# Cross-attention by pairs of feature chunks, with the null key taken out of the keys

## The reference, cut to what matters

```python
q = split_heads(layernorm(x) @ Wq) * DH ** -0.5
k, v = split(ctx @ Wkv)                      # then split_heads
k = concat(null_k, k); v = concat(null_v, v) # 129 keys
attn = softmax(q @ k.T)
out = merge_heads(attn @ v) @ Wout           # then a layer norm with scale and bias
x = x + tanh(g_xattn) * out
```

## Time and profile before

| | |
|---|---|
| runs | 588.56 us median of 3 (588.01 to 589.29) |
| profiled execution | span 586.1 us (its own device time is not listed apart from the runs) |
| TensorE matmul | 532.3 us busy, 91% |
| VectorE | 405.8 us busy, 69% |
| ScalarE | 308.6 us busy, 53% |
| GpSimd | 123.5 us busy, 21% |
| prologue | 0 to 50.7 us |
| groups 0 to 5 | 50.1 us each |
| group 6 | 42.0 us |
| group 7 | 39.1 us |
| feed-forward block | 432.5 us to the end |

### The profile page before, as it was taken

The page is one execution under the profiler, slowest core; times in us unless marked ns, Lnnn a source line. Parts: engine busy times, 40 slices in busy tenths (PEclk is TensorE's granted clock), DMA queues, the critical chain, the costliest instruction groups (busy, mean ns, idle before and its releaser), DMA issues. The chain is left out here.

```text
span 586.1 us, 11057 instructions
## 1 busy us (share of the span) xinstructions
PE 532.3 (91%) x3972; PEld 460.8 (79%) x3972; DVE 405.8 (69%) x1054; ACT 308.6 (53%) x880; POOL 123.5 (21%) x129
## 2 busy tenths in 40 slices
PE   2899999999999999999999999999678999807897
PEld 2888888888988998888898888887466878704797
DVE  4669844755574575466457447947785888999896
ACT  2744532643353363344335326425678659989992
POOL 3000310220130122022103102302303108940000
PEclk9999999999999999999999999999999999957999
DMA  7932001100110110010011001001300100010033
GB/s 243 350 127 73 2 1 55 37 2 3 52 36 0 54 36 0 20 41 28 0 54 36 0 1 37 1 2 56 107 19 2 36 0 2 0 36 1 1 102 115
DMA packets 18479, 25.88 MB, mean 44 GB/s; under 512 B 1216, under 2 KB 15808, under 8 KB 18448
## 3 DMA queue, kind: packets, MB, share of 16 engines
q1 hardware_dynamic: 18192, 25.17, 13.1%
q0 software_dynamic: 256, 0.30, 0.3%
HBM read 21.27 MB, written 4.19 MB: 43 GB/s over the span
## 5 line engine op out<-in xcount | busy, mean ns | idle before, releaser
L834 ACT ACTIVATE probs<-bank,nmax 128x129 f32<-128x129 f32 x256 | 91.0, 369 | 117.9 <-DVE nmax L1196 117.8
L1625 POOL TENSOR_TENSOR probs<-probs,rinv 128x512 f32<-128x512 f32 x64 | 66.7, 1043 | 339.0 <-DVE rinv L1204 339.0
L615 PE MATMUL bank<-wv,ctxT 128*128 128x512 f32 x384 | 94.3, 397 | 0.0
L607 PE MATMUL bank<-ctxT,wk 128*128 128x256 f32 x672 | 88.9, 282 | 0.0
L615 PEld LDWEIGHTS bank<-wv,ctxT 128*128 128x128 f32 x384 | 70.4, 188 | 17.0 <-issue 1.2
L607 PEld LDWEIGHTS bank<-ctxT,wk 128*128 128x128 f32 x672 | 83.6, 188 | 0.0
L1208 DVE COPY pT<-bank 128x512 f32<-128x512 f32 x64 | 43.7, 683 | 20.6 <-PE bank L678 18.7
L815 ACT ACTIVATE oT<-bank 128x256 fp32r<-128x256 f32 x64 | 24.8, 387 | 59.9 <-PE bank L687 59.9
L607 PE MATMUL bank<-xnT,wq 128*128 128x256 f32 x336 | 54.7, 298 | 0.0
L834 ACT ACTIVATION_READ_ACCUMULATOR probs<-bank,nmax 128x1 f32 x256 | 52.0, 203 | 0.0
L607 PEld LDWEIGHTS bank<-xnT,wq 128*128 128x128 f32 x336 | 43.2, 188 | 7.2 <-issue 1.2
(11 more groups left out here) (177 smaller groups left out, 846.5 us busy)
## 6 DMA issues: line engine op xcount, KB each, us to landing
craw<-in_ctx SPq DMA_DIRECT2D x8, 512.0 KB, 3.3
stage<-in_L_xattn_Wkv SPq DMA_DIRECT2D x8, 512.0 KB, 13.1
xa<-in_x SPq DMA_DIRECT2D x8, 256.0 KB, 2.7
xr<-in_x SPq DMA_DIRECT2D x8, 256.0 KB, 2.7
x_scratch<-y SPq DMA_DIRECT2D x7, 256.0 KB, 2.1
x2all<-x_scratch SPq DMA_DIRECT2D x1, 1792.0 KB, 8.4
xres<-x_scratch SPq DMA_DIRECT2D x6, 256.0 KB, 2.8
out<-yout SPq DMA_DIRECT2D x6, 256.0 KB, 2.2
```

The source lines that it names most:

```text
L607: last = mm(bk[:, n * TG:(n + 1) * TG], wt[a][:, k, f], act_t[b][:, k, :], start=(k == 0 and i == 0), stop=(k == kk - 1 and i == len(TERMS ...
L615: last = mm(bk[:, :], ctxT[a][:, k, b * S:(b + 1) * S], wv[w][:, k, h * 512:(h + 1) * 512], start=(k == 0 and i == 0), stop=(k == KC - 1 a ...
L834: last = nc.scalar.activation(probs[:, c % 2, u, 0:NK], score_bank[c % 2][h][:, b * QW:b * QW + NK], ACT.Exp, bias=nmax[:, c % 2, u:u + 1] ...
L1625: G.tensor_tensor(probs[:, c % 2, :, 0:S], probs[:, c % 2, :, 0:S], rinv[:, c % 2, :].rearrange("p (u o) -> p u o", o=1).to_broadcast([P, ...
```

## The change

A **pair** of chunks takes the place of a chunk (`NP = 4` pairs in a group). The null key is subtracted from every key when ScalarE copies the keys out of PSUM, so the score of the null key is 0 for every query and needs no column: four score tiles of 128 columns fill one bank, and the eight tiles of a pair fill two. TensorE makes the scores of a pair in one batch of 16 matmul instructions, the values of a pair in one batch into the whole of `pv_bank`, and the transposes in two halves `h`, each of four tiles, through the one `pt_bank`. `maxima` becomes, for each half, a reduce over 512 columns and a minimum with 0 that waits for it; `exps` gets a fifth small activation (the exponential of the null key); `inverse_sums` becomes an addition and a reciprocal that waits for it. A `Q` unit makes the keys first, and ScalarE copies its two halves with one activation each, the keys' with a bias.

The units are dealt anew into four slots of three parts, `ahead`, `between` and `behind` the two halves of the transposes; a unit may be cut in two (`"Q4<"`, `"Q4>"`). The rest of VectorE's list moves from eight steps to four slots.

```diff
-    PLAN = ([["Q0"], ["Q1"], ["Q2"], ["Q3"], ["Q4"], ["Q5", "V00"], ["Q6", "V10"], ["Q7", "X"]],
-            ["V01", "V11", "C", "W"])
-    PLAN_PENULT = ([["Q0"], ["Q1"], ["Q2"], ["Q3"], ["Q4"], ["V00"], ["Q5"], ["Q6"]], ["V10", "W"])
-    PLAN_FINAL = ([["V01"], ["V11"], ["Q7", "F0"], ["F1"], ["F2"], ["F3"], ["F4"], ["F5", "F6"]],
-                  ["F7", "F8", "W"])
+    PLAN = (((["Q0"], ["Q1"], ["Q2"]), (["Q3"], ["Q4<"], ["Q4>"]), (["Q5"], ["Q6"], ["V00"]),
+             (["Q7"], ["V10<"], ["V10>", "X"])), ["V01", "V11", "C", "W"])
+    PLAN_PENULT = (((["Q0"], ["Q1<"], ["Q1>"]), (["Q2"], ["Q3<"], ["Q3>"]), (["Q4"], ["Q5<"], ["Q5>"]),
+                    (["V00"], ["V10<"], ["V10>"])), ["W"])
+    PLAN_FINAL = (((["Q6"], ["Q7<"], ["Q7>"]), (["V01<"], ["V01>"], []), (["V11<"], ["V11>"], ["F0"]),
+                   (["F1"], ["F2", "F3"], ["F4", "F5"])), ["F6", "F7", "F8", "W"])
...
             def prob_transposes(g, p, h):
+                n = 2 * (g * NP + p) + h
+                pe.wait_ge(norm_done, n + 1)
+                wait(pe, pt_copied, n)
...
             def values(g, p):
+                wait(pe, pt_copied, 2 * (g * NP + p) + 2)
+                wait(pe, ot_lo, g * NP + p)
...
             def group(g):      # TensorE
+                for p in range(NP):
+                    if has_next(g, p):
+                        scores(*after_pair(g, p))
+                    ahead, between, behind = slots[p]
+                    run(ahead)
+                    prob_transposes(g, p, 0)
+                    run(between)
+                    prob_transposes(g, p, 1)
+                    run(behind)
+                    values(g, p)
+                run([u for u in tail if u != "C"])
...
             def exps(g, p, h):      # ScalarE
+                nc.scalar.activation(null_exp[:, p % 2, h, :], nmax[:, p % 2, h, :], ACT.Exp).then_inc(exp_done, 1)
...
             def attention_stats(g, dst):      # VectorE
-                maxima(g + 1, 1)
+                maxima(g + 1, 1, 0)
                 ln2.wait()
...
                 last.then_inc(w_free, 1)
+                maxima(g + 1, 1, 1)
...
+            def maxima(g, p, h):
+                n = 2 * (g * NP + p) + h + 1
+                if h == 0:
+                    dve.wait_ge(scores_done, g * NP + p + 1)
+                V.tensor_reduce(nmax[:, p % 2, h, :], score_bank[p % 2][h][:, :].rearrange("p (u s) -> p u s", s=S),
+                                AX.X, ALU.max, negate=True).then_inc(keys_max, 1)
+                dve.wait_ge(keys_max, n)
+                V.tensor_scalar(nmax[:, p % 2, h, :], nmax[:, p % 2, h, :], 0.0, None, ALU.min).then_inc(max_done, 1)
+            def inverse_sums(g, p, h):
+                n = 2 * (g * NP + p) + h + 1
+                dve.wait_ge(exp_done, n)
+                V.tensor_tensor(rowsum[:, p % 2, h, :], rowsum[:, p % 2, h, :], null_exp[:, p % 2, h, :],
+                                ALU.add).then_inc(total_done, 1)
+                dve.wait_ge(total_done, n)
+                V.reciprocal(rinv[:, p % 2, h, :], rowsum[:, p % 2, h, :]).then_inc(rinv_done, 1)
...
             def group(g):      # VectorE
+                for p in range(NP):
+                    if p:
+                        if has_next(g, p):
+                            for h in range(2):
+                                maxima(*after_pair(g, p), h)
+                        out_low(g, p - 1)
+                    ahead, between, behind = slots[p]
+                    if p == 0 and not first:
+                        attention_rstd(g - 1)
+                        attention_norm(g - 1, y)
+                    if p == 1 and not first:
+                        x2_statistics(g - 1, y[:, :, :])
+                    if p == 1 and feeds(g):
+                        ln_stats(g + 2)
+                    if p == 2 and feeds(g):
+                        ln_rstd()
+                    if first and p == 0:
+                        weight_values(0)
+                    if first and 1 <= p:
+                        (weight_scales, weight_integers, weight_values)[p - 1](1)
+                    if peeled and g == NG - 2 and 1 <= p:
+                        (weight_scales, weight_integers, weight_values)[p - 1](2)
+                    run(ahead)
+                    prob_copy(g, p, 0)
+                    if has_next(g, p):
+                        inverse_sums(*after_pair(g, p), 0)
+                    run(between)
+                    prob_copy(g, p, 1)
+                    if p == 2 and feeds(g):
+                        ln_apply()
+                    if has_next(g, p):
+                        inverse_sums(*after_pair(g, p), 1)
+                    run(behind)
```

More of the change, by code:

```diff
@@ L87, in gated_cross_attention_ffn @@
     NT = B * S // P
-    QW = S + 2
-    NK = S + 1
+    NP = NS // 2
     NBK = I * D // P // WBLOCK
@@ L159, in parity, with whole, after_pair, has_next @@
         return (len(PRO) + pos) % 2
+    def whole(part):
+        return [u for u in part if u[-1] != "<"]
+    def after_pair(g, p):
+        return (g, p + 1) if p + 1 < NP else (g + 1, 0)
+    def has_next(g, p):
+        return p + 1 < NP or not (isinstance(g, int) and g == NG - 1)
     def feeds(g):
@@ L659, in unit, with scores @@
                             last.then_inc(w_first, 1)
[L660 to L667, removed]
+                if half != 0:
+                    last.then_inc(unit_done, 1)
+            def scores(g, p):
+                if isinstance(g, int) and g == NG - 1 and p == NP - 1:
+                    unit_read(g, FINAL.index("Q7"))
+                wait(pe, exp_done, 2 * (g * NP + p) - 2)
+                for u in range(4):
+                    c, b = 2 * p + u // GB, u % GB
@@ L693, in _, with run @@
                 if PRO[pos] == "k6":
-                    pe.wait_ge(null_ready, 1)
                     scores(0, 0)
             def group(g):
[L698 to L715, removed]
+                pos, (slots, tail) = 0, plan(g)
+                def run(part):
+                    nonlocal pos
+                    for u in part:
+                        unit(g, pos, "<>".index(u[-1]) if u[-1] in "<>" else None)
+                        pos += u[-1] != "<"
+                for p in range(NP):
[9 more added lines that the diff above has]
+                run([u for u in tail if u != "C"])
             group(0)
@@ L1278, in _ @@
                 if PRO[npos[0]] == "k6":
-                    maxima(0, 0)
-                    inverse_sums(0, 0)
+                    for h in range(2):
+                        maxima(0, 0, h)
+                    for h in range(2):
+                        inverse_sums(0, 0, h)
                 if PRO[npos[0]] == "V11":
@@ L1283, in _ @@
                 npos[0] += 1
-            maxima(0, 1)
+            for h in range(2):
+                maxima(0, 1, h)
             dve.wait_ge(const_ready, 1)
@@ L1360, in group, with run @@
+                pos, (slots, tail) = 0, plan(g)
+                def run(part):
+                    nonlocal pos
+                    for u in whole(part):
+                        if u == "C":
+                            ctx_low(g + 2)
+                            continue
                         split(g, pos)
                         pos += 1
-                    if c < NS - 1 and weights:
-                        inverse_sums(g, c + 1)
-                    if c < NS - 1:
-                        prob_copy(g, c)
@@ L1386, in group @@
+                out_low(g, NP - 1)
+                run(tail)
                 if not final:
@@ L1638, in group @@
                                         ALU.add).then_inc(xgb_ready, 1)
-                    normalise(g, c)
-                if not (isinstance(g, int) and g == NG - 1):
-                    normalise(g + 1, 0)
+                    if has_next(g, p):
+                        for h in range(2):
+                            normalise(*after_pair(g, p), h)
             group(0)
```

250 lines of the change are left out of this document (107 added, 143 removed).

## The result

The changed kernel takes 612.32 us (median of 4 runs, 611.46 to 613.5) beside 588.28 us for the kernel before on the same chip: a ratio of 1.043 with a 95% interval of 1.041 to 1.045. The forecast was 606.6 us in a range of 596 to 614.

The account below looks back on a forecast made before the run. TensorE's own list was taken as the bound. Prologue +2.2, group 0 +3.4, loop groups +8.3, group 6 +2.9 and group 7 +1.2 sum to +18.0 on 586.1; with 2.5 for the median, 606.6 us, range 596 to 614.

Parts of the forecast that it names:

- What bounds the kernel, and the gain: TensorE's list sets the time up to 393 us; batching shortens a loop group by 2.64 us to 47.46.
- A unit behind transposes: On TensorE, a unit following transposes has no switch cost; bound 0.1 us each, 64 times, 6 us.
- The late copy: VectorE's first pT copy holds TensorE's second transposes: 2.1, 1.6, 0.6 us in slots 0, 1, 2; some 35 in all.
- The linked minimum: VectorE's minimum behind each reduction costs 0.21 us, a half 0.81; by the skill some 0.1 less.
- The waits of 2 us cost nothing in clock: TensorE's new waits leave the granted clock at 1.00, as in group 7 before with 6 us idle.
- The prologue: Softmax of a pair ahead of the value units' read-outs on VectorE adds 2.2 us (bounds 0 and 2.5).
- Group 7: The last group takes a Q unit and waits, partly offset by earlier idle time: +1.2 us (bounds -2 and +4).
- the first sign named: Sign that the forecast is right: a loop group lasts 51 to 52.5 us.
- (1): Rival: VectorE copies in time in slots 0 to 2 and the gain stands, 570 us; chance 0.08.
- (2): Rival: VectorE operations overlap more, halving the 35 us of waits in groups 0 to 6, about 589 us; chance 0.06.
- (3): Rival: ScalarE reloads its function table around each Q unit, delaying exps, 622 us; chance 0.03.
- (4): Rival: batches don't merge, each pair of score tiles on TensorE still pays its switch, 628 us; chance 0.02.

Follow-up runs that it names:

- third kernel: Changed kernel with the moved work of slots 0 to 2 and the weight quantisation of groups 0 and 6 put behind the second copies: 573.04 us, ratio 0.976.
- the first experiment: Changed kernel with only slot 0 altered: attention_rstd between VectorE's two pT copies, attention_norm behind the second: 597.26 us, ratio 1.016.
- the finer order: Against the kernel of 573.04 us: attention_rstd behind the second copy, second reciprocal later, quantisation spread, last group's second copy ahead of unit read-outs: 571.70 us, ratio 0.975.

## Why the prediction was right, and where it was off

**What bounds the kernel, and the gain.** Right. A loop group without waits was forecast at 47.46; with VectorE's list in order it is 47.7, so batching saves 2.4 us a group where 2.64 were worked out, and the batch cut in two shows that most of the saving is one of switches. 0.09 of the difference is a misread row: the 3.8 us of the earlier trace rows are not 0.48 in each of eight groups, but 1.04 in group 7 and 0.39 in the others. A unit behind transposes was taken at no switch cost: its first product starts 0.36 behind the first of four transposes (214.71 - 214.35), no more than four times 0.11, so it has none.

**The late copy.** Right in place and nearly in size. Lateness is counted here, as in the forecast, from when the next start was due; the idle time in the brackets of the rows is some 0.17 less, since a product's recorded end lies behind the start of the next one. The copy was forecast 7.23 after the start of slot 0 and 5.83 after that of slot 1; group 3 has 7.72 (218.74 - 211.02) and 5.80. The waits of slot 1 were forecast at 1.4 and 0.2 and measure 1.4 and 0.23, those of slot 2 at 0.6 and measure 0.5; the row that was to have "some 35 us in all" has 34.7. That these two agree so closely is in part luck: the 35 were the lateness of groups 0 to 6 with the waits of the values, the row has the idle time of all eight groups without them. Slot 0 was forecast at 2.1 and came to 2.3 to 2.8. Some 0.3 of that is, in groups 2 to 5, the idle time ahead of L1106 (0.30 to 0.33), where VectorE goes round the hardware loop; in groups 1 and 6, which it enters otherwise, the idle time is 0.02. I had read no price for that.

The linked minimum went as the rows said: with the minimum behind it one reduction follows the other after 0.80 (in slot 1 of group 3, from 224.49 to 225.29), where 0.81 was forecast. By the sentence that the prediction cites from the Trainium skill (VectorE: DVE Perf Modes, The DRAIN you can't avoid) it would be some 0.1 less. The page measured this on eight copies; the trace here does not agree for a small operation behind a large one, since the minimum starts 0.73 behind its reduction (225.22 - 224.49), and the measurement stands.

**The step that failed** is "The waits of 2 us cost nothing in clock". I had read it off group 7 of before, which has 6 us of idle TensorE at 1.00, but never looked how that idle time was cut up: it is six waits of 0.85 to 1.42. In groups 2, 4 and 5 the wait of slot 0 is followed by 3.41 us at a granted clock of 0.5, that is 1.2 GHz (in group 2 from 166.59 to 170.00). Group 2 of the changed kernel, TensorE behind the wait, and a window around that stretch:

```profile
165.76 0.63 PE L701 MATMUL bank<-ident,probs 128*128 128x128 f32 x4 [2.67 <-DVE pT L1255]
166.14 2.53 PE L627 MATMUL bank<-ctxT,wk 128*128 128x256 f32 x12
```

```profile
166.10:169.90 3.80, 3.80 (x23) 3.58 (x21) 0.94 (x3) 0.00 (x0) 1.96 (x2) 0.56 0.45 138
```

The 12 products that take 1.50 behind the wait of group 3 (219.95 to 221.45) take 2.33 here. Such a stretch costs some 1.7 us, three of them 5.1 of the 7.4 us by which groups 1 to 5 are over the forecast; the kernel with TensorE kept busy got 4.4 back in those groups. Of the other 2.3, about half is the gain of 2.4 in place of 2.64 (5 x 0.24 = 1.2), and the rest goes to the waits, of which slot 0's is the one that came out longer.

**The small terms.** The prologue came to +0.9 instead of +2.2. I can't say that the term was wrong: the same prologue ends between 50.3 and 53.2 in the profiles of the experiments, more than the term itself. What the term stands for is there: TensorE waits 1.5 us for VectorE's read-out of a value unit (1.52 at 41.44 in the changed kernel), which it does not do in the kernel before. Group 7 came to +0.3 instead of +1.2, within its bounds. So the total came within 6 us of the forecast in part because these terms were too high where the loop groups were too low. A loop group of 51 to 52.5, the first sign named, holds for groups 1 and 3 alone; the other three are above it by the clock.

**The rivals.** (1) "VectorE keeps up", 570, was wrong for the change as it is, and is what the kernel does once the work ahead of the first copy is behind the copies: 571. The first copy was the point that decided, as I had written. (2) falls with the 34.7 us, (3) and (4) fall with the rows above.

## What to carry to other kernels

When the engine that sets the time gets its work in larger batches, the others' lists in order have to be dealt anew by what frees its buffers: here the copy out of the one transpose bank had to come first and all side work behind it, 41 us between two orders of the same operations. The mean busy share of the second engine (60% of a group here, and 72% in the faster third kernel) says nothing about this; follow one slot from start to start. And price a long wait of TensorE twice, once for the wait and once for a stretch at half clock that may follow it.

## What the runs showed that I had not expected

- **The clock behind long waits.** Waits in which TensorE was idle for 2.1 to 3.1 us were in some cases followed by 3.41 us at 1.2 GHz and in others not: group 3 of the changed kernel has a wait as long as groups 4 and 5 and no fall, and its group 6 has none behind waits of 2.70 and 2.56. Shorter waits are no safe case: the waits of 1.3 to 1.8 in slot 1 of the loop groups were never followed by a fall, but in group 7 a wait of 1.38 with others close to it was, in the first experiment and in the one with the batches cut, while the finer order has the same wait of 1.38 and no fall. What decides between two equal waits stays open.
- **GpSimd holds up tiny operations of VectorE.** An operation on two columns took 1.05 us instead of 0.17 beside a multiplication of 1.04 that began with it. The Trainium skill (SBUF — State Buffer, Who interferes with whom) says that a VectorE operation with two inputs in SBUF, or in a mode that uses both ports, shares a port pair with GpSimd, and that whoever comes first keeps it for the whole instruction; the ends of these rows agree. So the place of an operation decides its price, and a row of another place bounds it only from below.
- **The end of a hardware loop** costs VectorE 0.30 to 0.33 us of idle time in groups 2 to 5 of the changed kernel, just where its work was most urgent.
